# A two-block image network on one core: the vector engine's copy of the attended values, moved behind the step's maximum and sum

## The chip, the core and the metric

The program runs on one NeuronCore of a Trainium2 chip. It is timed on the device, from launch to end, in microseconds. The core has five engines, each with its own instruction queue: TensorE (PE, matrix products and transposes; its weight loads are shown apart as PEld), VectorE (DVE), ScalarE (ACT), GpSimd (POOL) and SyncE (SP), which starts most transfers. Each engine takes its instructions strictly in the order in which they were written. Between engines the only order is that of semaphores: an instruction may wait until a counter has reached a value, and may raise one when it is done.

## What is computed

The input is a batch of 16 feature maps of 56 x 56 positions and 192 channels, float32. Two blocks follow each other, each with group normalization and a residual; the second one is windowed self-attention with a shifted window:

```
x = x + outlook(group_norm(x))        # first block: 3x3 weighted neighbourhood, 6 heads
x = x + windows(group_norm(x))        # second block
...
attn = einsum('wmqd,wmkd->wmqk', q * hd ** -0.5, k) + rpb + mask   # 12 heads, 49 x 49 in each 7 x 7 window
attn = softmax(attn)
out  = einsum('wmqk,wmkd->wqmd', attn, v) @ proj_weight.T + proj_bias
```

## The kernel before, in words

All five engines run a program written out by hand. A loop of eight passes (`NP`) takes two images each. Every pass has a **first stage** (seven chunks of the first block, `outlook`) and a **second stage**, the windowed attention, in which the change lies.

The second stage goes through eight **window rows** (w = 0 to 7), a row being the 8 windows side by side in each of the two images. A row has eight **steps** (s = 0 to 7). A step is worked on by four engines one after another, and different steps are in flight at once (`AHEAD` = 3), so that in step s:

- PE first transposes the finished probabilities of step s (`turn_probs`, L661), then computes the raw scores of step s+3 (`scores`, L632). In even steps it then multiplies the probabilities of the last two steps with the values (`attend`, L678), which leaves the attended values in the PSUM bank `Y_BANK`; and in every step a piece of the "ring" follows: projections for the next row (L299 to L309, L611 to L615), the output projection of the row before, or transposes for storing and loading (L696, L338).
- DVE adds the bias to the scores of step s+3 (`score_bias`, L1426 and L1429), takes their maximum over the keys (`score_max`, L1436), and takes the sum of the exponentials of step s+2 and its reciprocal (`prob_sum`, L1443 and L1446). In even steps there is also `keep_y` (L1451): it copies the attended values out of `Y_BANK` into the buffer `yt`. Some steps end with a piece of other work (`extras`: L1461, L1466, L1181, L1187).
- POOL subtracts the maximum (`shift_step`, L1645) for step s+3 and multiplies by the reciprocal (`normalize_step`, L1652) for step s+1; between them are pieces for other rows (L1631, L1638).
- ACT takes the exponential of step s+2 (L1047), copies the transposed probabilities of step s out of PSUM (`keep_probs`, L1057, twice a step) and evicts what the ring has computed.

PE transposes into the same bank `Y_BANK` from which `keep_y` copies. So in every odd step `turn_probs` may start only when the copy of the even step before it is done:

```
if s % 2 == 1:
    pe.wait_ge(y_kept, ONE + PAIRS * R + s // 2)
```

The last row, w = 7, differs from the others. There is no next row to project for, so the ring holds less PE work (`ring_last`), while DVE has more extras: statistics of the next images, the closing sums of the row before, and coefficients.

Of the kernel before, what the change touches and what calls it, by code (L numbers as in the profile page):

```python
# [64 lines left out]
PAIRS = NW // 2  # L65
# [19 lines left out]
def mixer(nc, x, wa, ba, wv, bv, wp, bp, wqkv, bqkv, wo, bo, table, sel_in, gmat_in, mask_in, out):  # L85
    ctx = ExitStack()
    with ctx:
# [124 lines left out]
        def ahead(w, s, n):  # L212
            return (w, s + n) if s + n < STEPS else (w + 1, s + n - STEPS)
# [957 lines left out]
        def _(dve):  # L1171
# [6 lines left out]
            def stat_x(image, c, tiles):  # L1178
                for j in tiles:
                    dve.wait_ge(x_kept, ONE + T * (CHUNKS * image + c) + j + 1)  # L1180
                    nc.vector.bn_stats(stats[:, j, c, :], xa[:, j, c * ROWS:(c + 1) * ROWS, 0:W]).then_inc(x_stat, 1)  # L1181

            def aggregate(g, stat, n):
                dve.wait_ge(stat, ONE + n)
                nc.vector.memset(fence[:], 0.0)
                for j in range(T):
                    nc.vector.bn_aggr(mv[:, j, :], stats[:, j, :, :].rearrange("p c s -> p (c s)")).then_inc(g_agg, 1)  # L1187

            def deviate(g, bank):
                dve.wait_ge(g_agg, ONE + T * (g + 1))  # L1190
                dve.wait_ge(g_mean, ONE + g + 1)
                tt(gdev[:], mv[:, :, 0], P[:, bank, 0:T], ALU.subtract).then_inc(g_dev, 1)
                nc.vector.tensor_copy(gmean[:], P[:, bank, 0:T]).then_inc(g_dev, 1)
                dve.wait_ge(g_dev, ONE + 3 * g + 2)
                tt(gdev[:], gdev[:], gdev[:], ALU.mult).then_inc(g_dev, 1)
                dve.wait_ge(g_dev, ONE + 3 * g + 3)
                tt(gsq[:], gdev[:], mv[:, :, 1], ALU.add).then_inc(g_sq, 1)

            def coefficients(g):
                dve.wait_ge(g_std, ONE + g + 1)  # L1200
                nc.vector.reciprocal(ga[:], gstd[:]).then_inc(g_rstd, 1)
                dve.wait_ge(g_rstd, ONE + g + 1)
                nc.vector.scalar_tensor_tensor(out=gb[:], in0=gmean[:], scalar=-1.0, in1=ga[:],
                                               op0=ALU.mult, op1=ALU.mult).then_inc(g_ready, 1)
# [87 lines left out]
            with dve.Fori(0, NP) as i:  # L1292
# [125 lines left out]
                def score_bias(w, s):  # L1418
                    S = STEPS * (NW * i + w) + s
                    m, b = s % 2, s % SOFTS  # L1420
                    kind = 2 * (w == NW - 1) + (s // 2 == PAIRS - 1)
                    two, one = (0, 2) if m == 0 else (2, 0)
                    dve.wait_ge(p_turned, ONE + 2 * (S - AHEAD))
                    dve.wait_ge(sc_mm, ONE + 2 * S + 1)
                    pair = lambda ap: ap.rearrange("p (a n) -> p a n", a=2)
                    tt(pair(sp_[:, b, 4 * N:8 * N]), P[:, one:one + 2, 0:2 * N],  # L1426
                       pair(relb[:, kind, 4 * N:8 * N]), ALU.add).then_inc(t_add, 1)
                    dve.wait_ge(sc_mm, ONE + 2 * S + 2)
                    tt(crossed(sp_[:, b, :]), P[:, two:two + 2, 0:4 * N].rearrange("p a (t n) -> p a t n", t=2),  # L1429
                       crossed(relb[:, kind, :]), ALU.add).then_inc(t_add, 1)  # L1430

                def score_max(w, s):
                    S = STEPS * (NW * i + w) + s
                    b = s % SOFTS
                    dve.wait_ge(t_add, ONE + 2 * S + 2)
                    red(mx[:, b, :], sp_[:, b, :].rearrange("p (h k) -> p h k", h=NH), AX.X,  # L1436
                        ALU.max).then_inc(t_max, 1)

                def prob_sum(w, s):
                    S = STEPS * (NW * i + w) + s  # L1440
                    b = s % SOFTS
                    dve.wait_ge(p_exp, ONE + S + 1)
                    red(sm[:, b, :], sp_[:, b, :].rearrange("p (h k) -> p h k", h=NH), AX.X,  # L1443
                        ALU.add).then_inc(p_sum, 1)
                    dve.wait_ge(p_sum, ONE + S + 1)
                    nc.vector.reciprocal(rc[:, b, :], sm[:, b, :]).then_inc(p_rec, 1)  # L1446

                def keep_y(w, p):
                    R = NW * i + w
                    dve.wait_ge(y_mm, ONE + STEPS * R + 2 * p + 2)  # L1450
                    nc.vector.tensor_copy(yt[:, w % 2, :, p * 2 * N:(p + 1) * 2 * N],  # L1451
                                          P[:, Y_BANK, 0:T * 2 * N].rearrange("p (j n) -> p j n", j=T)
                                          ).then_inc(y_kept, 1)

                def finish(w, n, bank):
                    R = NW * i + w
                    j = ORDER[n]
                    dve.wait_ge(out_mm, ONE + T * R + n + 1)
                    dve.wait_ge(xr_ok, ONE + T * (R + 1))
                    by_window = lambda ap: ap.rearrange("p (w r c) -> p w r c", r=WS, c=WS)  # L1460
                    tt(fin[:, j, SHIFT:SHIFT + RT].rearrange("p (r w c) -> p w r c", w=NW, c=WS), by_window(P[:, bank, 0:RT]),  # L1461
                       by_window(xr[:, w % 2, j, :]), ALU.add).then_inc(fin_ok, 1)
                    if n == T - 1:
                        dve.wait_ge(fin_ok, ONE + T * (R + 1))
                        wrap = lambda c: fin[:, :, c:c + RT].rearrange("p j (r n) -> p j r n", n=W)[:, :, :, 0:SHIFT]
                        nc.vector.tensor_copy(wrap(0), wrap(W)).then_inc(fin_wrap, 1)  # L1466

                def extras(w, s):
                    if 1 <= w < NW - 1:
                        if s == 4:  # L1470
                            finish(w - 1, 0, R0)
                            finish(w - 1, 1, R1)
                        elif s == 5:
                            finish(w - 1, 2, R0)
                        elif s == 6:
                            stat_x(i + 1, w - 1, (0, 1))
                        elif s == 7:
                            stat_x(i + 1, w - 1, (2,))
                    elif w == NW - 1:
                        if s == 1:  # L1480
                            stat_x(i + 1, w - 1, (0, 1))
                        elif s == 2:
                            stat_x(i + 1, w - 1, (2,))
                            aggregate(2 * i + 2, x_stat, T * CHUNKS * (i + 2))
                        elif s == 3:
                            finish(w - 1, 0, R0)
                            finish(w - 1, 1, R1)
                        elif s == 4:
                            finish(w - 1, 2, R0)
                            deviate(2 * i + 2, R1)  # L1490
                        elif s == 6:
                            coefficients(2 * i + 2)

                def window_row(w):
                    for s in range(STEPS):
                        w2, s2 = ahead(w, s, AHEAD)
                        if w2 < NW:
                            score_bias(w2, s2)
                        if s % 2 == 0 and s > 0:
                            keep_y(w, s // 2 - 1)  # L1500
                        elif s == 0 and w > 0:
                            keep_y(w - 1, PAIRS - 1)
                        if w2 < NW:
                            score_max(w2, s2)
                        w2, s2 = ahead(w, s, AHEAD - 1)
                        if w2 < NW:
                            prob_sum(w2, s2)
                        extras(w, s)

                for s in range(AHEAD):  # L1510
# [4 lines left out]
                for w in range(NW):  # L1515
                    window_row(w)

                w, Gn = NW - 1, CHUNKS * (i + 1)
# [218 lines left out]
```

## Time and profile before

| | |
|---|---|
| median of 3 runs | 3816.19 us (3811.17 to 3817.01) |
| the profiled execution, its own time | 3813.92 us |
| its span, first to last instruction | 3812.0 us |
| mean granted TensorE clock in it | 0.954 of full speed |
| PE busy | 90% |
| DVE busy | 72% |
| POOL busy | 63% |
| ACT busy | 50% |

Busy shares are means over stages that have different limits, so the stretch around the changed code has to be read by itself. A row of the time line is: start in us from the span's start, length in us, engine, line, operation, what is written <- what is read, how many instructions were merged, and in brackets how long the engine had been idle before it and what released it. Window rows are named by w, so the last one is row 7. The rows below are from the third of the eight passes; its window row 7 begins at 1434.97 us.

### The profile page before, as it was taken

What the parts mean: (1) busy time and instruction counts of PE and PEld (TensorE: products, weight loads), DVE (VectorE), ACT (ScalarE), POOL (GpSimd) and SP (SyncE); (2) the same over time, 40 slices, a digit from 0 to 9 for tenths busy, and PEclk for the clock granted to TensorE, in tenths of its full rate; (3) what the DMA queues carried; (4) which work ended last, traced back from release to release, by engine and by line L of the source; (5) the groups of instructions that cost most, each with busy time, mean ns of one, the idle gap of its engine ahead of it and who ended that gap; (6) DMA issues with size and microseconds to landing.
All of it is one profiled execution on the core that took longest, in us unless ns stands there. A gap on an engine that the chain in (4) does not pass through costs nothing.

```text
span 3812.0 us, 107668 instructions
## 1 busy us (share of the span) xinstructions
PE 3443.3 (90%) x39700; PEld 1940.6 (51%) x39700; DVE 2757.2 (72%) x4953; ACT 1913.3 (50%) x4042; POOL 2388.6 (63%) x1862
## 2 busy tenths in 40 slices
PE   3999989899798997999989899899998999989998
PEld 2346643466434664456634566335663456534665
DVE  2977759677596776967769677696777867687776
ACT  2445544456444664445643565435563456543565
POOL 0667737677375774767737677376764677556774
PEclk8999989899899998989989999899999999999999
DMA  3642217322273222722237122461224612155121
GB/s 79 128 90 71 79 42 142 79 67 78 55 140 73 70 72 68 140 63 78 68 77 142 49 74 74 86 129 58 72 67 96 124 54 78 56 116 106 58 75 58
DMA packets 206334, 317.58 MB, mean 83 GB/s; under 512 B 18904, under 2 KB 178136, under 8 KB 205784
## 3 DMA queue, kind: packets, MB, share of 16 engines
q0 software_dynamic: 31104, 148.65, 20.0%
q1 hardware_dynamic: 168992, 160.51, 14.3%
q8 instruction: 343, 5.62, 0.6%
q10 hardware_dynamic: 5688, 1.11, 0.2%
q14 instruction: 207, 1.70, 0.1%
HBM read 45.97 MB, written 38.54 MB: 22 GB/s over the span
## 4 chain that ended last, share of the span: by engine, by line
PE 59%; issue 11%; ACT 9%; DVE 8%; POOL 5%; DMA 4%; SPq 1%; ACTq 0%; DVEq 0%; POOLq 0%
PE P L678 5%; PE P L442 5%; PE P L661 4%; PE P L301 4%; PE P L299 4%; PE P L632 4%; PE P L308 3%; PE P L611 3%; DVE prod L1329 3%; DMA prod<-prod 3%; PE P L307 3%; PE P L696 2%; PE P L614 2%; PE P L302 2%; ACT kbd L1030 2%
## 5 line engine op out<-in xcount | busy, mean ns | idle before, releaser
L1645 POOL TENSOR_TENSOR sp__70<-sp__70,mx 128x588 f32<-128x588 f32 x512 | 600.8, 1174 | 611.5 <-DVE mx L1436 609.7
L1329 DVE TENSOR_TENSOR prod<-P,vpad 128x896 f32<-128x896 f32 (+1 forms) x768 | 790.4, 1049 | 138.3 <-PE P L442 122.1
L1652 POOL TENSOR_TENSOR sp__70<-sp__70,rc 128x588 f32<-128x588 f32 x512 | 601.1, 1175 | 13.0 <-DVE rc L1446 13.0
L1426 DVE TENSOR_TENSOR sp__70<-P,relb 128x196 f32<-128x196 f32 x512 | 184.4, 360 | 526.9 <-PE P L632 526.9
L1057 ACT ACTIVATE pt<-P 98x294 f32<-98x294 f32 x1024 | 430.9, 422 | 200.0 <-PE P L661 197.3
L1565 POOL DMA_DIRECT2D prod<-prod x216 | 202.5, 940 | 488.1 <-DVE prod L1329 484.5
L442 PE MATMUL P<-at,sel 108*128 108x448 bf16 x1512 | 428.4, 362 | 61.9 <-DVE prod L1329 33.0
L661 PE MATMUL P<-ident,sp__70 113*98 113x113 f32 x3072 | 400.8, 268 | 43.3 <-POOL sp__70 L1652 34.7
L661 PEld LDWEIGHTS P<-ident,sp__70 113*98 113x98 f32 x3072 | 331.7, 132 | 141.7 <-POOL sp__70 L1652 66.1
L1436 DVE TENSOR_REDUCE mx<-sp__70 128x12 f32<-128x588 f32 x512 | 389.6, 761 | 9.4
L1047 ACT ACTIVATE sp__70<-sp__70 128x588 f32<-128x588 f32 x512 | 360.5, 704 | 58.7 <-POOL sp__70 L1645 58.0
L1443 DVE TENSOR_REDUCE sm<-sp__70 128x12 f32<-128x588 f32 x512 | 386.9, 756 | 0.6
L442 PEld LDWEIGHTS P<-at,sel 108*128 108x128 bf16 x1512 | 113.0, 98 | 434.3 <-issue 232.7
L632 PE MATMUL P<-kbd,qs 32*64 32x98 f32 x12288 | 302.7, 262 | 19.9 <-DVE sp__70 L1429 14.4
L1581 POOL TENSOR_TENSOR psum_p<-psum_p,prod 128x1344 f32<-128x1344 f32 x96 | 300.4, 3129 | 8.0 <-DVE prod L1329 3.0
L1429 DVE TENSOR_TENSOR sp__70<-P,relb 128x392 f32<-128x392 f32 x512 | 284.2, 555 | 0.0
L1041 ACT ACTIVATE vs<-P 98x192 f32<-98x192 f32 x512 | 128.1, 333 | 265.4 <-PE P L611 265.4
L632 PEld LDWEIGHTS P<-kbd,qs 32*64 32x64 f32 x12288 | 202.6, 132 | 106.6 <-issue 78.2
L678 PE MATMUL P<-pt,vbd 98*32 98x49 f32 x12288 | 221.0, 218 | 32.7 <-ACT pt L1057 19.3
L1638 POOL TENSOR_SCALAR xr<-xa,bout 128x392 f32<-128x392 f32 x192 | 247.1, 1288 | 0.0
L976 ACT ACTIVATE xa<-P,bias 128x448 f32<-128x448 f32 x168 | 107.5, 640 | 257.1 <-PE P L460 218.1
L1581 POOL TENSOR_TENSOR psum_p<-prod 128x1344 f32<-128x1344 f32 x56 | 172.5, 3080 | 81.8 <-DMA prod<-prod 81.8
(223 smaller groups left out, 7401.4 us busy)
## 6 DMA issues: line engine op xcount, KB each, us to landing
prod<-prod POOLq DMA_DIRECT2D x216, 672.0 KB, 5.5
vbd<-vs SPq DMA_DIRECT2D x512, 147.0 KB
xin<-in_x SPq DMA_DIRECT2D x126, 336.0 KB, 4.0
out<-ot SPq DMA_DIRECT2D x184, 168.0 KB, 2.3
out<-ot SPq DMA_DIRECT2D x80, 84.0 KB
wn<-in_L_conv_qkv_weight SPq DMA_DIRECT2D x2, 432.0 KB, 6.7
wno<-in_L_conv_proj_weight SPq DMA_DIRECT2D x2, 144.0 KB, 6.8
self<-in_sel ACTq DMA_DIRECT2D x3, 91.1 KB
```

The lines of the kernel that those rows point to most:

```text
L442: last = mm(P[:, 2 * (n % 2) + b, 0:CT], sel[:, k, :], at[:, col:col + CT], start=True, stop=True)
L632: last = mm(P[half * SLOT:(half + 1) * SLOT, r, part * 2 * N:(part + 1) * 2 * N], qs[rows, w % 2, j, tok:tok + SLOT], kbd[rows, w % 2, j, ...
L661: last = turn(P[0:2 * N, bank, c * QUERIES:(c + 1) * QUERIES], sp_[0:QUERIES, s % SOFTS, g * 2 * N:(g + 1) * 2 * N], ident[0:QUERIES, 0:QU ...
L678: last = mm(P[32 * r:32 * r + 32, Y_BANK, col:col + N], vbd[w % 2][:, 2 * p + half, m, 2 * HD * g:2 * HD * (g + 1)], pt[:, (q + m) % KEPT, ...
L1047: go(sp_[:, s % SOFTS, :], sp_[:, s % SOFTS, :], ACT.Exp).then_inc(p_exp, 1)
L1057: go(pt[:, (STEPS * w + s) % KEPT, 3 * b:3 * b + 3, :, :], src, ACT.Copy).then_inc(p_kept, 1)
L1329: tt(by_row(dst), by_row(P[:, b:b + len(op), 0:CT]), val, ALU.mult).then_inc(prod_ok, 1)
L1436: red(mx[:, b, :], sp_[:, b, :].rearrange("p (h k) -> p h k", h=NH), AX.X, ALU.max).then_inc(t_max, 1)
L1443: red(sm[:, b, :], sp_[:, b, :].rearrange("p (h k) -> p h k", h=NH), AX.X, ALU.add).then_inc(p_sum, 1)
L1581: tt(y0[:] if n == PADD - 1 else psum_p[:], slot(0) if n == 0 else psum_p[:], slot(k), ALU.add).then_inc(padd_ok, 1)
L1645: tt(per_head(sp_[:, b, :]), per_head(sp_[:, b, :]), spread(mx[:, b, :]), ALU.subtract).then_inc(t_sub, 1)
L1652: tt(per_head(sp_[:, b, :]), per_head(sp_[:, b, :]), spread(rc[:, b, :]), ALU.mult).then_inc(p_norm, 1)
```

## The change

In an even step, `keep_y` stood between `score_bias` and `score_max` of the vector engine's program. It now stands behind `prob_sum`, ahead of `extras`. Nothing else is edited; the same instructions with the same waits are issued.

```diff
                         if w2 < NW:
                             score_bias(w2, s2)
-                        if s % 2 == 0 and s > 0:
-                            keep_y(w, s // 2 - 1)
-                        elif s == 0 and w > 0:
-                            keep_y(w - 1, PAIRS - 1)
                         if w2 < NW:
                             score_max(w2, s2)
                         w2, s2 = ahead(w, s, AHEAD - 1)
                         if w2 < NW:
                             prob_sum(w2, s2)
+                        if s % 2 == 0 and s > 0:
+                            keep_y(w, s // 2 - 1)
+                        elif s == 0 and w > 0:
+                            keep_y(w - 1, PAIRS - 1)
                         extras(w, s)
```

How this moves instructions is shown at two places of DVE's queue. `sp__70` is the tile of scores, `mx`, `sm` and `rc` its maximum, sum and reciprocal, `relb` the bias; REGISTER_ALU and ISA rows only prepare or hold waits. The first place is step 0 of the last window row, from behind its `score_bias`; steps 0 of the other rows (but the first) read the same. Before:

```order
L1451 COPY yt<-P 128x3x98
L1436 TENSOR_REDUCE mx<-sp__70 128x12
L1442 REGISTER_ALU
L1443 TENSOR_REDUCE sm<-sp__70 128x12
L1446 RECIPROCAL rc<-sm 128x12
```

and in the changed kernel:

```order
L1436 TENSOR_REDUCE mx<-sp__70 128x12
L1442 REGISTER_ALU
L1443 TENSOR_REDUCE sm<-sp__70 128x12
L1446 RECIPROCAL rc<-sm 128x12
L1451 COPY yt<-P 128x3x98
```

Three busy instructions that stood behind the copy now stand ahead of it. The second place is step 2 of the last window row, where extras follow. Before:

```order
L1429 TENSOR_TENSOR sp__70<-P,relb 128x2x2x98
L1451 COPY yt<-P 128x3x98
L1436 TENSOR_REDUCE mx<-sp__70 128x12
L1442 REGISTER_ALU
L1443 TENSOR_REDUCE sm<-sp__70 128x12
L1446 RECIPROCAL rc<-sm 128x12
L1180 REGISTER_ALU
L1181 BN_STATS stats<-xa 128x6
```

and in the changed kernel:

```order
L1429 TENSOR_TENSOR sp__70<-P,relb 128x2x2x98
L1436 TENSOR_REDUCE mx<-sp__70 128x12
L1442 REGISTER_ALU
L1443 TENSOR_REDUCE sm<-sp__70 128x12
L1446 RECIPROCAL rc<-sm 128x12
L1451 COPY yt<-P 128x3x98
L1180 REGISTER_ALU
L1181 BN_STATS stats<-xa 128x6
```

The copy passes the same three instructions and stays ahead of the extras. PE's, ACT's, POOL's and SP's queues are the same in both kernels.

## Rows read from the trace of the kernel before

**Rows 1.** The page, its first part: span, and busy time by engine.

```profile
span 3812.0 us, 107668 instructions
...
PE 3443.3 (90%) x39700; PEld 1940.6 (51%) x39700; DVE 2757.2 (72%) x4953; ACT 1913.3 (50%) x4042; POOL 2388.6 (63%) x1862
```

**Rows 2.** The copy's line L1451: lengths; its waits; who waited for it.

```profile
L1451 DVE COPY yt<-P x256: 450/465/468, 275.1 to 3789.2; 128x294 f32<-128x294 f32 x128
...
  PE P L678: 129.7, 111
...
  PEld P L661: 4.3, 16
```

**Rows 3.** Waits of the whole execution: total us, times, longest.

```profile
PE P L661 <- POOL sp__70 L1652: 34.7, 33, 2.1
```

**Rows 4.** Time line of DVE in window rows 3 and 4, third pass.

```profile
1330.01 0.23 DVE L1446 RECIPROCAL rc<-sm 128x12 f32<-128x12 f32 x1
1330.15 1.12 DVE L1181 BATCH_NORM_STATS2 stats<-xa 128x6 f32<-128x448 f32 x2
...
1335.48 0.56 DVE L1429 TENSOR_TENSOR sp__70<-P,relb 128x392 f32<-128x392 f32 x1
...
1339.74 0.56 DVE L1429 TENSOR_TENSOR sp__70<-P,relb 128x392 f32<-128x392 f32 x1
1340.34 0.77 DVE L1436 TENSOR_REDUCE mx<-sp__70 128x12 f32<-128x588 f32 x1
1341.02 0.76 DVE L1443 TENSOR_REDUCE sm<-sp__70 128x12 f32<-128x588 f32 x1
1341.81 0.23 DVE L1446 RECIPROCAL rc<-sm 128x12 f32<-128x12 f32 x1
```

**Rows 5.** Time line of PE: row 3, step 3; row 4, step 1.

```profile
1314.75 0.54 PE L696 MATMUL P<-ident,fin 128*112 128x128 f32 x3 [1.04 <-ACT pt L1057]
...
1338.26 0.74 PE L661 MATMUL P<-ident,sp__70 113*98 113x113 f32 x6
```

**Rows 6.** Time line of DVE in the last window row, steps 0 and 2.

```profile
1436.50 0.56 DVE L1429 TENSOR_TENSOR sp__70<-P,relb 128x392 f32<-128x392 f32 x1
...
1443.62 0.56 DVE L1429 TENSOR_TENSOR sp__70<-P,relb 128x392 f32<-128x392 f32 x1
1444.11 0.47 DVE L1451 COPY yt<-P 128x294 f32<-128x294 f32 x1
```

**Rows 7.** Time line of PE in the last window row, steps 0 to 5.

```profile
1434.97 0.79 PE L661 MATMUL P<-ident,sp__70 113*98 113x113 f32 x6
...
1438.59 0.78 PE L661 MATMUL P<-ident,sp__70 113*98 113x113 f32 x6 [0.65 <-POOL sp__70 L1652]
...
1444.01 0.54 PE L696 MATMUL P<-ident,fin 128*112 128x128 f32 x3
1444.63 0.79 PE L661 MATMUL P<-ident,sp__70 113*98 113x113 f32 x6
...
1450.48 0.93 PE L307 MATMUL P<-yt,mid 128*128 128x392 f32 x2 [0.34 <-DVE fin L1461]
...
1453.73 0.76 PE L661 MATMUL P<-ident,sp__70 113*98 113x113 f32 x6
1455.18 0.96 PE L696 MATMUL P<-ident,fin 128*112 128x128 f32 x6 [0.68 <-DVE fin L1466]
```

**Rows 8.** Time line of PE's weight loads in the last window row.

```profile
1434.97 0.56 PEld L661 LDWEIGHTS P<-ident,sp__70 113*98 113x98 f32 x6 [0.45 <-POOL sp__70 L1652]
...
1444.63 0.56 PEld L661 LDWEIGHTS P<-ident,sp__70 113*98 113x98 f32 x6 [0.33 <-DVE yt L1451]
```

**Rows 9.** Time line of POOL, window row 6, step 6.

```profile
1430.06 1.17 POOL L1645 TENSOR_TENSOR sp__70<-sp__70,mx 128x588 f32<-128x588 f32 x1 [2.34 <-DVE mx L1436]
```

**Rows 10.** PE in the first window row, step 5; then busy time, clock by stretch.

```profile
1220.51 0.79 PE L661 MATMUL P<-ident,sp__70 113*98 113x113 f32 x6 [2.10 <-POOL sp__70 L1652]
...
1222.00:1232.00 10.00, 8.03 (x95) 6.02 (x96) 5.13 (x11) 2.49 (x7) 6.68 (x7) 0.51 0.14 45
```

## The prediction

> **What bounds the kernel now.** I read the page first, then the wait lists, then the time lines of DVE, PE and POOL over the second stage of the third pass. The page says PE: 90% busy, DVE 72%, POOL 63% [rows 1]. A faster vector step is therefore worth nothing by itself; it counts only where PE waits for what DVE makes, at first or second hand. There are two such paths around the copy, and they pull in opposite directions.
>
> The path that the change shortens goes from the maximum over POOL's subtraction, the exponential, the sum and POOL's normalization to PE's transposes (L661). PE waited for POOL there 33 times, 34.7 us in all [rows 3]. DVE itself sat 129.7 us in front of the copy, waiting for PE's product [rows 2], and the maximum of every even step stood behind that.
>
> The path that the change lengthens is short: copy, semaphore, PE's transposes of the next odd step, which write the bank that the copy reads. PE's weight loads waited for it only 16 times, 4.3 us in all [rows 2]. That is two places per pass, and one of them is shown: the copy that starts at 1444.11 takes 0.47 us, and PE's weight load for step 3 starts at 1444.63, after 0.33 us of waiting [rows 6, 8]. So at step 2 of window row 7 PE already starts the moment the copy lets it, 0.05 us behind its end. Anything that delays this copy delays PE one for one.
>
> **How late the copy becomes.** Start from the second bias addition (L1429), whose start does not depend on the moved copy within its own step. In a step without a copy the maximum starts 0.60 us after it, the sum another 0.68, the reciprocal another 0.79 (1339.74, 1340.34, 1341.02, 1341.81) [rows 4], and whatever follows the reciprocal starts 0.14 us later (1330.01, 1330.15) [rows 4]. The copy then takes 0.465 us [rows 2] and PE sees it 0.05 us later [rows 6, 8]. From the start of L1429 to the weight load that is 0.60 + 0.68 + 0.79 + 0.14 + 0.47 + 0.05 = 2.73 us. Before it was 1444.63 - 1443.62 = 1.01 us.
>
> **Window rows 1 to 6.** PE has a long piece of the ring between the product and the next transposes, and this covers the delay almost exactly. At step 0 of row 4 the addition starts at 1335.48 [rows 4] and PE's transposes at 1338.26 [rows 5], 2.78 us later; the weight load is now ready at 2.73. A weight load that comes in front of a waiting PE costs about 0.05 us more than one made early: the transposes took 0.79 us right after a wait and 0.74 without one [rows 5, 7]. So the margin is zero. Six rows in eight passes are 48 such steps, at 0 to 0.05 us each, 0 to 2.4 us in all; I take 0.02 each, 1.0 us, because the sum of the steps meets PE's start and does not pass it. What step 2 may lose is swallowed one step later, where PE waits 1.04 us for ACT in any case [rows 5]. At step 4 DVE used to wait for PE's product before the copy, so that the maximum can go first for nothing, and step 6 has a longer ring piece: both cost nothing. If the cover here were gone by 0.1 us more than I think, it would be 48 x 0.1 = 4.8 us.
>
> **Window row 7.** There the ring piece behind the product is short. In order:
>
> 1. Entering the row, something is gained. POOL's subtraction in step 6 of row 6 had been idle 2.34 us for the maximum [rows 9], which stood behind a copy; POOL then runs without a pause up to the normalization for which the weight load at 1434.97 waited 0.45 us [rows 8]. The maximum starts where the copy started, so it comes about 0.36 us earlier. The weight load needs 0.13 us ahead of the matmul, so at most 0.32 us can be had; I take 0.30. Step 0 starts at 1434.67.
> 2. Step 0 to 1. L1429 starts at 1436.50 - 0.30 = 1436.20, the weight load can start at 1436.20 + 2.73 = 1438.93, against 1438.59 before, when it waited for POOL [rows 6, 7]. PE is now 0.34 us behind.
> 3. Step 2 to 3. L1429 of step 2 follows PE, at 1443.62 + 0.34 = 1443.96; the weight load is ready at 1446.69 against 1444.63 [rows 6, 8]. PE is 2.06 us behind. Its last work before was at 1444.01 + 0.54 + 0.34 = 1444.89 [rows 7], so that it stands idle 1.80 us where it was idle 0.08.
> 4. Step 4. PE used to wait 0.34 us for DVE's first closing sum [rows 7]. With PE 2.06 late that sum is ready, so 2.06 - 0.34 = 1.72 us remain. The copy of step 4 is behind the sum as well, but PE's transposes come at 1453.73 + 1.72 = 1455.45, about a microsecond after it. The 0.68 us wait at 1455.18 [rows 7] gives nothing back: the second half of those transposes needs ACT's copy of the probabilities of step 5, which has moved with PE.
>
> From there to the end of the pass DVE and POOL wait for PE (DVE's next copy is one wait for the product), so the 1.72 us stay. Row 7 comes 8 times: 8 x 1.72 = 13.8 us. The bounds of this term: if the entry gain were zero it is 8 x 2.0 = 16 us; if in step 3 the row's other waits took half a microsecond more, 8 x 1.2 = 9.8 us.
>
> **The sum.** 13.8 + 1.0 = 14.8 us on the profiled execution's own 3813.92, which makes 3828.7. That execution lies 2.3 us under the median of the three runs, 3816.19; on the median it is **3831 us**, 0.39% slower. About 0.2%, 7.6 us, is what a measurement of this kernel can tell from no change.
>
> **Rivals.**
>
> *The clock falls in the new gap (3843 us and more).* In the first window row PE waited 2.10 us for POOL, then 1.6 us once more, and the stretch that followed ran at a granted clock of 0.51, that is 1.2 instead of 2.4 GHz [rows 10]. The new idle of 1.80 us lies in a row with smaller gaps around it. If the clock fell there in all passes for 3 us, a third of that stretch of 10 us, half of them would be lost, 8 x 1.5 = 12 us, 3843 us; for 10 us it would be 8 x 5 = 40 us, 3871 us. I take the short one, since PE is busy from step 3 on and row 0 is not. Against it: the gap is shorter than the one in rows 10, and stands alone. It decides once PE's idling there goes above some 2 us.
> The Trainium skill, in "TensorE: Matmul & The Clock Gate", section "HAM oscillation — how this bites in real kernels", says that waits between bursts of matmuls throw the array back to the half clock and that this is paid again at each such wait. By that rule the time would be this rival's 3843 us, not the sum's 3831; the trace agrees that it happens after waits, at 0.51, but shows it for a longer wait only.
>
> *No change (3816 us).* The 1.72 us could be given back later in each pass, where ACT, DVE and PE wait for each other at the end of the row. For it: the tail is full of waits. Against it: they follow PE's own order, and PE is what comes late. It decides if the first wait that PE meets after step 5 is for something that did not follow PE and exceeds 1.7 us.
>
> *Faster (3806 us).* The maximum leaves the 129.7 us of waiting [rows 2] behind. If at the one place of each pass where this wait is longest, step 6 of row 0, the earlier maximum let PE start some 1.2 us earlier, that is 8 x 1.2 = 9.6 us, and it wins if also the copy in row 7 is not what PE waits for (its price would be zero, for instance if a different semaphore were last). It needs PE to be waiting on that chain within the next steps; of the 34.7 us [rows 3] the largest piece, 2.10 us a pass [rows 10], belongs to POOL waiting for PE's value products, not for a maximum. Little speaks for it.
>
> **How the numbers follow.** The forecast as worked out, 3824 to 3838: 0.62. The clock rival, above 3838: 0.14. No change: 0.14. Faster: 0.10. So slower by over 0.2% 0.76, within 0.2% 0.14, faster 0.10. The range that leaves out 2 in 10 begins at 3818, inside "no change", and ends at 3848, inside the clock rival; the likeliest case's own range is 3824 to 3838.
>
> **What the profile afterwards would show.** Right: in row 7 of each pass PE's weight loads for steps 1 and 3 wait for `yt` (L1451), 16 more waits in the list, with 0.3 to 1.0 us at step 1 and about 1.8 us at step 3; the wait of PE for DVE's closing sum at step 4 is gone; the wait of DVE in front of the copy (129.7 us) is largely gone, and nothing comes of it; rows 1 to 6 are as long as before to within 0.1 us each. Wrong: no wait on `yt` at step 3, or one of under 1 us (then my 2.73 us does not hold in the full queue); rows 1 to 6 longer by more than 0.1 us each (then the margin of zero is really negative); a granted clock near 0.5 between steps 3 and 5 of row 7 (the first rival); or a row 0 that is shorter (the last).

## The result

| | before | after |
|---|---|---|
| median | 3813.68 us (3810.8 to 3817.01, 4 runs) | 3848.39 us (3843.9 to 3848.86, 4 runs) |
| the profiled execution | 3813.92 us | 3848.86 us |
| mean granted TensorE clock in it | 0.954 | 0.946 |

The changed kernel is slower: the ratio is 1.0089, with a 95% interval of 1.0077 to 1.0101. The medians differ by 34.7 us, where the prediction had summed up 14.8 us; 3848.39 lies 17 us above the forecast of 3831 and 0.4 us above the upper end of the range, 3848.

The page of the kernel after, its first part, answers to [rows 1]:

```profile
span 3847.0 us, 107668 instructions
...
PE 3469.7 (90%) x39700; PEld 1958.1 (51%) x39700; DVE 2753.9 (72%) x4953; ACT 1911.5 (50%) x4042; POOL 2384.7 (62%) x1862
```

The span is 35.0 us longer, and PE is busy 26.4 us more with the same 39700 matmuls. Waits alone can't do that, since a waiting PE is not busy. Three quarters of the loss look like matmuls that took longer, which is the first hint at the clock.

The copy's line in the trace after, with its lengths, its waits and who waited for it, answers to [rows 2]:

```profile
L1451 DVE COPY yt<-P x256: 398/401/466, 277.4 to 3824.5; 128x294 f32<-128x294 f32 x128
...
  PE P L678: 101.4, 17
...
  PEld P L661: 63.7, 115
  PE P L661: 24.4, 16
```

The last two lines must be read together. PE's weight loads now wait for the copy 115 times instead of 16, but in only 16 of these does PE itself stand still, 24.4 us in all. A weight load overlaps the matmuls ahead of it, and its wait costs nothing while they run. The line also shows that DVE lost 94 of its 111 waits for PE's product, yet only 28 of their 129.7 us. The two long ones of each pass, at the end of row 7, stay (5.4 and 7.3 us in the third pass), and the shorter of them was only 3.5 us there before: PE now comes later.

DVE in the last window row of the third pass, steps 0 and 2, answers to [rows 6]. The row now begins at 1441.93:

```profile
1443.42 0.56 DVE L1429 TENSOR_TENSOR sp__70<-P,relb 128x392 f32<-128x392 f32 x1
...
1445.48 0.23 DVE L1446 RECIPROCAL rc<-sm 128x12 f32<-128x12 f32 x1
1445.62 0.40 DVE L1451 COPY yt<-P 128x294 f32<-128x294 f32 x1
...
1451.12 0.56 DVE L1429 TENSOR_TENSOR sp__70<-P,relb 128x392 f32<-128x392 f32 x1
1451.71 0.77 DVE L1436 TENSOR_REDUCE mx<-sp__70 128x12 f32<-128x588 f32 x1
1452.39 0.76 DVE L1443 TENSOR_REDUCE sm<-sp__70 128x12 f32<-128x588 f32 x1
1453.18 0.23 DVE L1446 RECIPROCAL rc<-sm 128x12 f32<-128x12 f32 x1
1453.33 0.40 DVE L1451 COPY yt<-P 128x294 f32<-128x294 f32 x1
```

PE in the same row, steps 1 to 6, answers to [rows 7]:

```profile
1446.08 0.79 PE L661 MATMUL P<-ident,sp__70 113*98 113x113 f32 x6 [1.18 <-DVE yt L1451]
...
1451.37 0.54 PE L696 MATMUL P<-ident,fin 128*112 128x128 f32 x3
1453.78 0.79 PE L661 MATMUL P<-ident,sp__70 113*98 113x113 f32 x6 [1.87 <-DVE yt L1451]
...
1456.80 1.59 PE L301 MATMUL P<-yt,wot 128*128 128x392 f32 x2
...
1460.83 0.93 PE L307 MATMUL P<-yt,mid 128*128 128x392 f32 x2
...
1464.08 0.76 PE L661 MATMUL P<-ident,sp__70 113*98 113x113 f32 x6
1465.13 1.70 PE L696 MATMUL P<-ident,fin 128*112 128x128 f32 x6 [0.29 <-ACT pt L1057]
1466.62 2.98 PE L316 MATMUL P<-gsq,gm 128*128 128x1 f32 x14
```

From the start of the addition to PE's transposes it is 1446.08 - 1443.42 = 2.66 us and 1453.78 - 1451.12 = 2.66 us, against 1.01 us before at step 3. PE stands idle 1.18 us at step 1 (predicted: 0.3 to 1.0) and 1.87 us at step 3 (predicted: about 1.8), and the wait in front of L307 is gone, as predicted. Then come two things that are not waits. Behind the second gap two matmuls of L301, with nothing ahead of them to wait for, take 1.59 us; and the output transposes of step 5 (L696) take 1.70 us against 0.96 before [rows 7]. In the kernel before, L301 and the products of one column behind the output transposes (L316) took, in the same pass:

```profile
1446.72 0.93 PE L301 MATMUL P<-yt,wot 128*128 128x392 f32 x2
...
1455.98 1.62 PE L316 MATMUL P<-gsq,gm 128*128 128x1 f32 x14
```

Busy time and clock by stretch of the kernel after show why they are longer:

```profile
1441.90:1453.70 11.80, 8.52 (x212) 6.63 (x210) 9.77 (x22) 7.83 (x20) 9.16 (x9) 1.00 0.45 141
1453.70:1458.20 4.50, 4.42 (x36) 2.36 (x37) 3.79 (x11) 1.30 (x3) 2.61 (x4) 0.62 0.03 9
1458.20:1465.00 6.80, 6.64 (x107) 4.53 (x105) 5.64 (x14) 1.72 (x5) 3.15 (x3) 1.00 0.01 1
1465.00:1481.90 16.90, 12.84 (x140) 9.57 (x142) 2.17 (x6) 9.47 (x19) 2.00 (x3) 0.50 0.14 39
```

The columns are: stretch, length, busy time (and instructions) of PE, PEld, DVE, ACT and POOL, granted clock, share of the DMA engines and GB/s. The clock is at its full level, 2.4 GHz, up to the gap, falls to 1.2 GHz for most of the 4.5 us behind it (0.62 as a mean over both levels), rises while PE works almost without a pause, and falls again at 1465.0, as the output transposes of step 5 begin.

This holds for every pass. Step 3 begins 11.85 us into the row. In all eight passes the clock fell 11.4 to 12.8 us into the row, so shortly before or behind the end of the gap, for some 3 us in five passes and some 7 us in three. Before, it stayed high there and first fell 21.6 to 23.0 us into the row, at the end of step 5 or the start of step 6.

For the account I took the length of each step, from the first transposes (L661) of one to those of the next, in both traces, and subtracted. There are no such transposes between row 7 and the row 0 of the next pass, so step 7 of row 7 as counted here is some 204 us long: it holds the rest of row 7 and the whole first stage of the next pass. Summed over the eight passes, in us:

| stretch | after - before |
|---|---|
| last step of row 6 | -2.3 |
| row 7, step 0 | +4.3 |
| row 7, step 1 | -1.0 |
| row 7, step 2 | +14.3 |
| row 7, step 3 | +16.8 |
| row 7, step 4 | -2.9 |
| row 7, step 5 | +9.9 |
| row 7, steps 6 and 7, with the next pass's first stage | -5.9 |
| all other steps of rows 1 to 6 | +0.7 |
| row 0, start and end | +1.1 |
| sum | +35.0 |

Without steps 3 and 5 to 7, row 7 and its entry come to 12.4 us. These are the waits that the prediction summed at 13.8. Steps 3 and 5, where the clock was low, add 16.8 and 9.9 us. The stretch behind them takes 5.9 us off, some 2.3 up to the last output transposes of row 7 and 3.6 in the next pass's first stage, and 1.8 us lie elsewhere. In the other kernels of this document the part in the first stage differs from the kernel before by anything from -5.3 to +5.0 us, so no cause can be read from it. The 0.7 us of rows 1 to 6 are one step of one pass (step 2 of row 2, the last pass); all other steps of these rows are as before to 0.06 us.

### The profile page after: what moved, and what is told of

Its sections match the earlier page's. It is cut to its first block, busy times and chain, and to the rows that moved or that the text cites. A ratio compares the mean times of both kernels' runs of the same rounds, so it can differ in the third digit from the quotient of the medians.

```text
span 3847.0 us, 107668 instructions
## 1 busy us (share of the span) xinstructions
PE 3469.7 (90%) x39700; PEld 1958.1 (51%) x39700; DVE 2753.9 (72%) x4953; ACT 1911.5 (50%) x4042; POOL 2384.7 (62%) x1862
## 4 chain that ended last, share of the span: by engine, by line
PE 62%; issue 10%; ACT 9%; DVE 8%; DMA 5%; POOL 3%; SPq 1%; ACTq 0%; DVEq 0%; POOLq 0%
PE P L661 5%; PE P L678 5%; PE P L442 4%; PE P L301 4%; PE P L299 4%; PE P L632 4%; PE P L611 3%; PE P L308 3%; DMA prod<-prod 3%; DVE prod L1329 3%; PE P L307 3%; PE P L614 3%; PE P L696 2%; PE P L302 2%; PE P L612 2%
## 5 line engine op out<-in xcount | busy, mean ns | idle before, releaser
L661 PE MATMUL P<-ident,sp__70 113*98 113x113 f32 x3072 | 404.3, 270 | 60.3 <-POOL sp__70 L1652 29.2
L661 PEld LDWEIGHTS P<-ident,sp__70 113*98 113x98 f32 x3072 | 331.9, 133 | 161.7 <-DVE yt L1451 63.7
```

Source lines behind the costliest of these rows:

```text
L661: last = turn(P[0:2 * N, bank, c * QUERIES:(c + 1) * QUERIES], sp_[0:QUERIES, s % SOFTS, g * 2 * N:(g + 1) * 2 * N], ident[0:QUERIES, 0:QU ...
```

## The experiments

My theory after the result: 12 us are waits in the last row, nearly all made by the copy of step 2; the gap that it leaves drops the clock, and this costs about as much again; and because step 5 comes later, it falls under the low clock that came behind it before. The rival: the step-3 loss is no matter of the clock but of the late copy itself (a queue that has drained, a bank that is still in use), or the loss comes from many rows, each a little. "Before" below is the median of the kernel before on the same chip, and every interval is one of 95%. All nine kernels use one small helper, called twice in the step; only in the shorter delay below does the second call stand elsewhere:

```diff
+                def keep_if(w, s, now):
+                    if now and s % 2 == 0 and s > 0:
+                        keep_y(w, s // 2 - 1)
+                    elif now and s == 0 and w > 0:
+                        keep_y(w - 1, PAIRS - 1)
...
                         if w2 < NW:
                             score_bias(w2, s2)
+                        early = ...            # differs
+                        keep_if(w, s, early)   # where the copy stood before
...
                             prob_sum(w2, s2)
+                        keep_if(w, s, not early)   # where the change puts it
```

### Which rows

The change in all rows but the last:

```diff
+                        early = w == NW - 1
```

> The copy stands behind the sum in window rows 1 to 6 and ahead of the maximum, as before, in row 7 alone. Theory A (the whole loss arises in row 7, where PE's ring piece is short and the weight loads of steps 1 and 3 wait for the copy): the time is that of the kernel before less the gain on entering row 7, some 0.3 us in each of 8 passes, so 3811 us, and ratio 0.9985 to 1.0005. Theory B (the later copy costs a little in each of some 200 places, and row 7 only shows it most): at least half of the 35 us stays, 3830 us or more.

Measured: 3815.22 us, before 3814.22, ratio 1.0004 (0.9995 to 1.0013). The steps of rows 1 to 6 are as long as before to 0.07 us, except the last one of row 6, where the gain of 0.29 us a pass stays (2.3 us in all). Steps 0 to 4 of row 7 are as before to 0.1 us. So all copies but the four of the last row can stand at either place. The 2.3 us do not appear in the total because step 5 of row 7 and the stretch from step 7 on became 3.8 and 2.9 us longer; 3.4 us of the former lie in two passes in which the clock fell 19.7 us into the row and not 21.6 or later. I expected 3811 and missed that.

Only the last row:

```diff
+                        early = w < NW - 1
```

> The reverse: the copy stands behind the sum in row 7 alone, and ahead of the maximum in all other rows. Theory A: the whole loss is there and the entry gain is gone, since the maximum of step 6 of row 6 stands behind a copy again: 3849 to 3852 us. Theory B: under half of the loss, 3830 us or less.

Measured: 3856.62 us, before 3814.22, ratio 1.0109 (1.0095 to 1.0123). Four copies of a pass make all of the loss, and more of it than the whole change: step 3 costs 21.7 us instead of 16.8, since the low clock lasted some 7 us in seven of eight passes. The rest of the difference is the entry gain, which is gone (2.3 us), and the stretch from step 7 on, which is 2.8 us longer than before instead of 5.9 shorter. PE's time line at step 3, third pass:

```profile
1459.39 1.37 PE L661 MATMUL P<-ident,sp__70 113*98 113x113 f32 x6 [1.88 <-DVE yt L1451]
```

and the stretch from there, of the same kernel:

```profile
1459.30:1466.20 6.90, 6.81 (x40) 3.77 (x41) 4.39 (x13) 1.30 (x3) 3.46 (x4) 0.51 0.02 6
```

The gap is the same as after the change (1.88 and 1.87 us), but here the clock is low already for the transposes right behind it, which take 1.37 us instead of 0.79. The same idle time can cost 1.6 or 3.0 us.

### Which step of the last row

The copy moved in one single step of each pass, step 2 of the last row:

```diff
+                        early = not (w == NW - 1 and s == 2)
```

> The copy stands behind the sum in step 2 of row 7 alone, one copy of 32 in a pass. By theory A and C nearly all of the loss hangs on this one: the copy makes PE wait 1.6 to 1.8 us more (about 1.3 us a pass stay after step 4, 10 us in all), and if the clock falls behind that wait as in the changed kernel, step 3 adds 13 to 22 us: 3835 to 3852 us. If a wait that is a tenth of a microsecond shorter is under what the clock forgives, step 3 stays at 3.5 us and the time is 3825 us. Theory B gives under 3817 us.

Measured: 3847.86 us, before 3815.46, ratio 1.0087 (1.0074 to 1.0101), which is the whole change's. By step: step 2 +13.2 us, step 3 +15.3, step 4 -2.5, step 5 +9.8, step 7 with the next first stage -8.0. Time line of PE at step 3, third pass:

```profile
1451.63 0.79 PE L661 MATMUL P<-ident,sp__70 113*98 113x113 f32 x6 [1.74 <-DVE yt L1451]
```

and the stretch behind, of the same kernel:

```profile
1452.90:1456.40 3.50, 3.50 (x9) 1.53 (x8) 2.70 (x6) 0.56 (x2) 1.81 (x2) 0.51 0.00 0
```

PE is busy for all of these 3.5 us, and gets 1.2 GHz. One instruction of 0.47 us, moved behind three others once a pass, costs 32 us.

Its counterpart, only step 0:

```diff
+                        early = not (w == NW - 1 and s == 0)
```

> The copy stands behind the sum in step 0 of row 7 alone. PE is held 0.5 to 0.6 us there and 0.1 us comes back at step 1; no long idle follows, so no clock term: 8 x 0.45 = 3.6 us less whatever the waits of step 2 and step 4 give back, 3815 to 3819 us, which the measurement can hardly tell from the kernel before. If the clock term hangs on the number of small waits in the row and not on the one long wait, it shows here: step 3 or 4 longer than before, 3822 us or more.

Measured: 3822.43 us, before 3815.46, ratio 1.0018 (1.0009 to 1.0027). PE of this kernel in row 7, steps 1 and 5, third pass:

```profile
1441.34 0.79 PE L661 MATMUL P<-ident,sp__70 113*98 113x113 f32 x6 [1.22 <-DVE yt L1451]
...
1458.69 2.01 PE L316 MATMUL P<-gsq,gm 128*128 128x1 f32 x14
```

The gap of 1.22 us at step 1 did not bring the clock down: steps 3 and 4 are as before to 0.1 us. But the time is above the 3815 to 3819 that I expected from the waits. Steps 0 to 2 cost 4.4 us, and step 5 another 3.5: it starts 0.5 us later after the row's start, so that more of it lies behind the fall of the clock, which came 21.8 to 22.8 us into the row; L316 takes 2.01 us instead of 1.62. That branch of the expectation that I had kept for a fall at step 3 or 4 gave the right size for a wrong reason.

### A shorter delay

The copy between the maximum and the sum, in all rows:

```diff
                             score_max(w2, s2)
+                        keep_if(w, s, not early)   # early = False
                         w2, s2 = ahead(w, s, AHEAD - 1)
```

> The copy stands between the maximum and the sum in all rows. By the same steps as the prediction the weight load can start 0.60 + 0.68 + 0.40 + 0.05 = 1.7 us behind L1429 instead of 2.66. Theory A: step 0 of row 7 is then not held by the copy (POOL is later), the entry gain of 0.3 us stays, step 2 is held 0.4 to 0.7 us longer than before, no wait reaches 1 us, and the clock does not fall at step 3: 3811 to 3819 us. If the loss goes by how many instructions stand ahead of the copy in every row (theory B), about a third to a half of it stays: 3825 to 3835 us.

Measured: 3814.49 us, before 3814.22, ratio 1.0000 (0.9991 to 1.0009). PE at step 3, third pass:

```profile
1441.90 0.79 PE L661 MATMUL P<-ident,sp__70 113*98 113x113 f32 x6 [0.87 <-DVE yt L1451]
```

PE still waits, 0.87 us, and step 2 costs 6.3 us; step 4 returns 3.2 and the entry gain 2.3. The clock does not fall in steps 3 and 4, and nothing is lost. With step 2 held 0.78 us longer a pass instead of 1.78, the cost is not in proportion smaller: none of it can be measured.

### The gap filled

If the step-3 loss is the clock's, then work for PE in the gap must remove it, although the copy comes as late as after the change. The kernel after, and at the end of PE's step 2 in the last row fourteen products of constants into a free PSUM bank, which no result uses:

```diff
+                            if s == 2:
+                                pe.wait_ge(ot_kept, ONE + NT * (NW * i + w - 2) + 3)
+                                for _ in range(14):
+                                    mm(P[:, R1, 0:256], identb[0:QK * SPLITS, :],
+                                       sel[:, 0:2, :].rearrange("p k n -> p (k n)"), start=True, stop=True)
```

> The changed kernel, with 14 matmuls of 256 columns into a free bank at the end of PE's step 2 of row 7; they add work that no result uses and fill most of the 1.87 us in which PE waits for the copy. Theory C (about half of the loss is TensorE's clock, which fell to half behind this wait in every pass): the granted clock stays at full speed through steps 3 and 4, step 3 is 3.5 us long again instead of 5.1 to 6.5, and the time is 3828 to 3836 us. Rival D (the length of step 3 comes from the late copy itself, through banks or through DVE, and the clock only happens to fall there): step 3 stays longer than 5 us and the time stays within 3 us of 3848.

Measured: 3835.44 us, before 3814.22, ratio 1.0055 (1.0041 to 1.0069). PE of this kernel at steps 2 to 4, third pass:

```profile
1445.51 0.54 PE L696 MATMUL P<-ident,fin 128*112 128x128 f32 x3
1445.88 1.69 PE L829 MATMUL P<-sel,identb 108*128 108x256 bf16 x14
1447.92 0.79 PE L661 MATMUL P<-ident,sp__70 113*98 113x113 f32 x6 [0.35 <-DVE yt L1456]
...
1451.43 0.74 PE L661 MATMUL P<-ident,sp__70 113*98 113x113 f32 x6
```

and the clock of step 3 and behind:

```profile
1448.00:1453.00 5.00, 5.00 (x100) 3.27 (x102) 4.89 (x14) 2.38 (x6) 3.11 (x3) 1.00 0.02 4
```

Step 2 is as late as after the change, +14.3 us in both, so the added work did not change how late step 3 begins. Step 3 is now as long as before, +0.0 instead of +16.8, at a clock of 1.00. This is the one comparison in which the lateness is the same and only PE's idleness differs, and it settles the question between clock and lateness. In the total 13 us are won, not 16.8, since the stretch from step 5 to the next row 0 now costs 10.0 us instead of 4.0: the clock falls 21.6 to 23.1 us into the row, as before the change.

To see whether these 10 us are the clock's too, six such products more, ahead of the output transposes of step 5:

```diff
+                        if w == NW - 1 and s == 5:
+                            pe.wait_ge(t_add, ONE + 2 * STEPS * NW * (i + 1))
+                            for _ in range(6):
+                                mm(P[:, 0, 0:256], identb[0:QK * SPLITS, :],
+                                   sel[:, 0:2, :].rearrange("p k n -> p (k n)"), start=True, stop=True)
```

> e3_warm with 6 more matmuls of 256 columns into a free bank at step 5 of row 7, ahead of the transposes for the output; again no result uses them. e3_warm kept 21 us of the loss, of which its waits explain 12 and step 5 another 10: group_variances there ran at the low clock. Theory E (step 5 is longer because the clock falls earlier against the row's work): the clock falls after group_variances, step 5 is back at 3.7 us or less plus the added work, 3825 to 3830 us. Rival F (step 5 is longer because it waits for ACT): the added work changes nothing or costs its own 0.3 us a pass, 3835 to 3838 us.

Measured: 3823.45 us, before 3815.46, ratio 1.0023 (1.0014 to 1.0032). PE of this kernel in step 5, third pass:

```profile
1457.24 0.82 PE L819 MATMUL P<-sel,identb 108*128 108x256 bf16 x6
...
1458.88 1.62 PE L316 MATMUL P<-gsq,gm 128*128 128x1 f32 x14
```

and the clock of that step:

```profile
1457.00:1461.40 4.40, 4.01 (x37) 3.48 (x34) 1.36 (x5) 4.08 (x9) 2.00 (x3) 1.00 0.20 54
```

Step 5 goes from +10.3 to -1.7 us, and the clock first falls 25.4 to 26.5 us into the row, behind step 5. L316, fourteen products of one column, takes 1.62 us here, 2.01 in the kernel with only step 0 moved, and 2.98 after the change. With both falls of the clock kept away, 8.5 us remain on the span: about 12.0 us of waits, less 3.9 us that the stretch from step 5 to the next row 0 now gains on the kernel before, and 0.4 us elsewhere.

### The margin of rows 1 to 6

The prediction had the margin of the copy at zero there, and these rows lost nothing. How far were they from losing? Row 7 as before, and ahead of the moved copy at step 0 of rows 1 to 6 a memset of 160 columns into a buffer of its own:

```diff
+                        if 0 < w < NW - 1 and s == 0:
+                            nc.vector.memset(pad[:], 0.0)
                         keep_if(w, s, not early)
```

> Row 7 as before; rows 1 to 6 with the copy behind the sum, and at step 0 of each of them the copy comes later still by a memset of 160 elements of an otherwise unused buffer (about 0.2 us), which stands ahead of it. In the changed kernel the copy of step 0 ended 0.17 us ahead of PE's transposes, 0.05 of it the semaphore: a margin of some 0.1 us. If that cover is what made rows 1 to 6 free, each of the 48 steps gets 0.05 to 0.15 us longer, 2 to 7 us in all: 3816 to 3821 us. If PE does not depend on the copy in these rows at all, their steps stay as they are.

Measured: 3819.71 us, before 3815.46, ratio 1.0010 (1.0001 to 1.0019). DVE of this kernel, third pass:

```profile
1333.81 0.19 DVE L1514 MEMSET pad<- 128x160 f32 x1
1333.92 0.40 DVE L1452 COPY yt<-P 128x294 f32<-128x294 f32 x1
```

The memset moved the copy by only 0.17 us (it starts 0.32 us behind the reciprocal's start instead of 0.15), and step 0 of these rows became 0.06 us longer each (0.15 in row 1), 3.5 us in all. So the margin is 0.1 us: the cover is thin, but it is not negative.

### The two gains without the loss

The entry gain needs only rows 0 to 6 changed, and the second filler holds the clock in step 5 in any order. Together: the order of the first experiment, and the six products of step 5.

> The order of e1_last_row_as_before (copy behind the sum in rows 1 to 6, ahead of the maximum in row 7) with the 6 added matmuls of 256 columns at step 5 of row 7 from e8_warm_twice, whose results nothing uses. If the clock's fall moves from about 22.5 us to 25 us or more after the row's start, as it did there, steps 5 and 6 of the row run at full speed: 8 x 0.3 to 0.5 us, on top of the 2.3 us of the entry gain, 3808 to 3812 us, possibly faster than both kernels. If in this order the clock falls where it did, or comes back later for it, the added 0.3 us a pass is all that is left: 3815 to 3819 us.

Measured: 3808.37 us, before 3814.71, ratio 0.9984 (0.9975 to 0.9993). It beats both kernels, if by little. PE of this kernel in step 5, third pass:

```profile
1454.25 1.62 PE L316 MATMUL P<-gsq,gm 128*128 128x1 f32 x14
```

Steps 5 and 6 are 1.7 and 3.3 us shorter than before and the entry keeps its 2.3 us; in seven of eight passes the clock now falls only 28.9 to 30.1 us into the row, in step 7. The stretch from step 7 on gives 5.7 us back, but just 0.7 of them before the last output transposes of row 7. The other 5.0 lie in the next pass's first stage, and why is not shown.

## Why the prediction fell short

The direction and the waits were right; the size was not. That 3848.39 lies only 0.4 us above the range is no merit of the sum: the range reached that far because the clock rival had its share in it.

**The delay of 2.73 us: right.** 2.66 us in both steps. The difference is the copy, which takes 0.40 us right behind the reciprocal and not the 0.465 of [rows 2], taken behind a tensor_tensor or after idle time.

**Rows 1 to 6, 1.0 us: nothing in seven passes, 0.7 us once in the eighth.** The shorter copy made the zero margin one of 0.1 us. The step was priced right within its bounds. The sign "rows 1 to 6 unchanged" came true.

**Row 7, the waits, 13.8 us: right, 12.4 us.** Per pass, predicted and the median measured: entry gain 0.30 and 0.29; step 2 makes the lateness 1.72 larger, and measured 1.78; step 4 gives 0.34 back, and measured 0.40; PE's idle before step 3 was 1.80 and is 1.87 us. "So the 1.72 us stay" was about right for the waits: 12.4 / 8 is 1.55.

**The step that failed is the one that took the clock out of the sum.** The rival had the place, the mechanism and nearly the price (half of 3 us, 1.5 us a pass; measured 1.60 in five passes and 2.8 to 3.0 in three, 16.8 us in all). It stood outside the forecast, with a chance of 0.14, on the argument that it "decides once PE's idling there goes above some 2 us". That number came from the only row of a fall that I had shown, 2.10 us [rows 10], and such a row gives no lower bound: it says that 2.10 us was enough in its place, not that 1.80 us is too little. Nor did it need "then 1.6 us once more": in the trace of the kernel before the clock fell 0.2 to 3.0 us behind the end of the 2.10 us in all eight passes, in three of them ahead of the second wait. The same trace has 40 idle times of 1.04 us (step 3 of rows 2 to 6, [rows 5] shows one) and no fall at any of them, so it left everything between 1.04 and 2.10 us open. The runs put the point lower than 2.10. With 1.74, 1.87 and 1.88 us the clock fell; with 1.22 us (step 1), 0.87 us (the copy in the middle) and 0.35 us (the gap filled) it did not. A gap of nearly the size of that in [rows 10] should have had at least an even chance of the fall. The Trainium skill, in "TensorE: Matmul & The Clock Gate", section "HAM oscillation — how this bites in real kernels", describes a kernel in which TensorE waits some 3 to 5 us for DMA between bursts of matmuls, begins the next burst at the half clock, and pays for this at every such wait. The trace agrees for the gap of 1.87 us at step 3, which was followed by the half clock in eight passes of eight (0.62 as a mean over the 4.5 us in the third) though it is shorter than the waits of that section; at the 1.18 us of step 1 the clock stayed at 1.00. The prediction's "by that rule" left out how long the waits of that section are.

**Step 5 "gives nothing back": right as to the wait, but it cost 9.9 us.** The prediction followed waits only, and treated the rest of the pass as shifted by 1.72 us as a whole. But in the kernel before the clock falls at the end of that step or just behind it, 21.6 to 23.0 us into the row, and the fall did not move along with the work. In the third pass step 5 begins 1464.08 - 1441.93 = 22.15 us into the row, and began 1453.73 - 1434.97 = 18.76 us into it before [rows 7]; the clock falls at 23.1 us, so that nearly the whole step comes under it (L696 1.70 us for 0.96, L316 2.98 for 1.62 before). In the fifth pass the clock fell only 26.3 us into the row, behind step 5, and there the step was as long as before. The stretch from step 7 on returned 5.9 us. No rival of the prediction covers this. Measured is that this fall comes at the same time into the row in the kernel before and in the one with the filled gap (21.6 to 23.1 us), though step 5 begins 1.8 us later there. After the change it comes at 23.0 to 23.1 us in four passes and at 25.0 to 26.3 us in the other four, with step 5 beginning 3.4 to 5.0 us later. Why it comes when it does is not shown.

**The signs.** The 16 waits of PE came, with 1.18 and 1.87 us against "0.3 to 1.0" and "about 1.8"; of the weight loads' waits there were 99 more, not 16, and the others, 96 of them at two steps in each of rows 1 to 6, cost nothing. The wait of step 4 is gone. DVE's wait in front of the copy was to be "largely gone": 94 of 111 went, but only 28 of 129.7 us.

What stays open is why the same gap costs 1.6 us in one pass and 3.0 in another, which is one reason why the last row alone (3856.6 us) is slower than the whole change (3848.4 us). Three kernels with this gap give 24 passes. In ten of them the clock fell 0.8 to 1.4 us after PE had resumed, and step 3 became 1.6 us longer in all ten. In the other fourteen it fell earlier, down to half a microsecond before PE resumed, and step 3 became 2.5 to 3.05 us longer in twelve and 1.6 us in two. The moment of the fall thus goes with the price, but no run varied it by itself. The length of the low level goes with it in all 24: some 3 us in the twelve passes that lost 1.6 us, some 7 us in the twelve that lost 2.5 to 3.05.

## What to carry to other kernels

When a change makes PE wait, price the clock as well as the wait: look in the trace for every idle stretch of similar length and whether the clock fell behind it, and if there is only a fall to go by, take it as likely for the shorter gap too. Here the waits cost 12 us and the low clock more than that, for one copy of 0.4 us placed badly once a pass. An instruction that releases a bank for PE goes ahead of reductions that nobody is waiting for soon, in the stages where PE's own queue has little work to cover it; and where a gap can't be avoided, products in it that nobody needs may keep the clock, as 1.7 us of them did here.

## What the runs showed of the hardware

- PE idle once for 1.74 to 1.88 us, in a row with a pause of about 1.2 us or 0.65 us some 7 us earlier, was followed by 1.2 GHz in each of 24 passes; so was 2.10 us in row 0, in each of 8 of the kernel before, with a wait of up to 1.6 us close behind. Idle times of 1.22, 1.18, 1.04 and 0.87 us were not. Fourteen products of 256 columns in the gap, 1.69 us, prevented it.
- The fall came between 0.5 us before and 1.4 us after the gap's end, and the low level lasted up to 7 us while PE worked without a pause. It cost 1.6 us a pass where it lasted some 3 us, and 2.5 to 3.05 where it lasted some 7.
- The same copy of 128 x 294 from PSUM took 0.40 us right behind a reciprocal of 128 x 12 or a memset of 128 x 160, and 0.46 to 0.47 behind a tensor_tensor of 128 x 392 or after DVE had been idle. I had priced both at 0.465.
- A memset of 0.19 us put into DVE's queue moved the next instruction by 0.17 us.
